# Other places for moments, factor transfers, first maximum and first turned x1 in an adaLN block's prologue

## The reference, cut to what matters

```python
mod = (silu(c) @ wmod).reshape(B, 6, 1, -1)
sa, ca, ga, sb, cb, gb = (mod[:, i] for i in range(6))
ga, gb = (2 * (g >= 0) - 1) * maximum(abs(g), 0.25)     # each gate
h = layernorm(x) * (1 + ca) + sa
q, k, v = h @ Wq.T, h @ Wk.T, h @ Wv.T                  # rank 64 shared by the heads
x = x + ga * (softmax(q @ k.T) @ v) @ Wo.T
h = layernorm(x) * (1 + cb) + sb
x = x + gb * ((h @ sum(factors)) / sqrt(8) + bias)      # 8 factors of 512 x 512
```

## Time and profile before

| | us |
|---|---|
| median of 3 runs (471.33 to 473.3) | 471.39 |
| profiled execution | 475.28 |
| its span | 473.2 |
| TensorE matmuls busy | 453.5 (96%) |
| VectorE busy | 365.2 (77%) |
| ScalarE busy | 332.1 (70%) |
| GpSimd busy | 249.9 (53%) |

### The profile page before, as it was taken

The page is one execution under the profiler, slowest core; times in us unless marked ns, Lnnn a source line. Parts: engine busy times, 40 slices in busy tenths (PEclk is TensorE's granted clock), DMA queues, the critical chain, the costliest instruction groups (busy, mean ns, idle before and its releaser), DMA issues.

```text
span 473.2 us, 7421 instructions
## 1 busy us (share of the span) xinstructions
PE 453.5 (96%) x2114; PEld 365.3 (77%) x2114; DVE 365.2 (77%) x627; ACT 332.1 (70%) x662; POOL 249.9 (53%) x317
## 2 busy tenths in 40 slices
PE   8999887989999999999999999999999999999996
PEld 3776666868888888888888888888888876777675
DVE  2896783779888778788888878888887668897665
ACT  2877735667887778687878777887877457657551
POOL 0476653535155565456464645555554466566662
PEclk9999998999999999999999999999999999999999
DMA  8968788673358646687867365777776246665612
GB/s 298 387 233 228 151 158 193 111 134 109 97 166 265 190 135 201 188 257 194 265 187 246 112 206 174 236 216 215 225 217 160 69 132 187 194 195 166 201 61 91
DMA packets 78199, 88.06 MB, mean 186 GB/s; under 512 B 4936, under 2 KB 55880, under 8 KB 78160
## 3 DMA queue, kind: packets, MB, share of 16 engines
q1 hardware_dynamic: 74208, 80.00, 54.6%
q0 software_dynamic: 3808, 7.34, 9.3%
q10 hardware_dynamic: 144, 0.26, 0.2%
HBM read 53.49 MB, written 34.10 MB: 185 GB/s over the span
## 4 chain that ended last, share of the span: by engine, by line
PE 75%; DVE 7%; issue 6%; ACT 4%; DMA 3%; POOL 3%; SPq 0%; ACTq 0%; DVEq 0%; POOLq 0%
PE ps_o L449 11%; PE ps_o L451 11%; PE ps_o L450 11%; PE ps_y L450 5%; PE ps_y L449 5%; PE ps_y L451 5%; PE ps_v L449 5%; PE ps_v L450 5%; PE ps_v L451 5%; PE ps_s L523 3%; PE ps_s L524 3%; PE ps_qk L449 2%; PE ps_t L455 2%; PE ps_qk L451 2%; PE ps_qk L450 2%
## 5 line engine op out<-in xcount | busy, mean ns | idle before, releaser
L1321 POOL TENSOR_SCALAR ve<-mv 128x1 f32<-128x1 f32 x64 | 23.4, 365 | 162.3 <-DVE mv L1077 114.3
L449 PE MATMUL ps_o<-v_lo,pt_hi 128*128 128x512 f32 x256 | 100.2, 391 | 2.4 <-DVE pt_lo L966 2.3
L450 PE MATMUL ps_o<-v_hi,pt_lo 128*128 128x512 f32 x256 | 99.7, 389 | 0.0
L451 PE MATMUL ps_o<-v_hi,pt_hi 128*128 128x512 f32 x256 | 99.6, 389 | 0.0
L966 DVE TENSOR_TENSOR h_lo<-h_f,h_hi 128x512 fp32r<-128x512 f32 (+1 forms) x67 | 51.8, 772 | 12.7 <-ACT h_hi L685 12.2
L449 PEld LDWEIGHTS ps_o<-v_lo,pt_hi 128*128 128x128 f32 x256 | 48.1, 188 | 14.7 <-issue 4.8
L451 PEld LDWEIGHTS ps_o<-v_hi,pt_hi 128*128 128x128 f32 x256 | 48.1, 188 | 10.1
L450 PEld LDWEIGHTS ps_o<-v_hi,pt_lo 128*128 128x128 f32 x256 | 48.0, 188 | 9.6
L714 ACT ACTIVATE h_f<-x1b,mod_t 128x128 f32<-128x128 f32 x120 | 53.0, 596 | 1.0 <-DVE x1b L1095 0.7
L449 PE MATMUL ps_y<-f_lo,h_hi 128*128 128x512 f32 (+1 forms) x124 | 48.5, 391 | 1.8 <-issue 1.0
L450 PE MATMUL ps_y<-f_hi,h_lo 128*128 128x512 f32 (+1 forms) x124 | 47.9, 386 | 0.0
(11 more groups left out here) (181 smaller groups left out, 1033.2 us busy)
## 6 DMA issues: line engine op xcount, KB each, us to landing
x_blocks<-xn SPq DMA_DIRECT2D x50, 256.0 KB, 2.5
p_blocks<-probs SPq DMA_DIRECT2D x24, 512.0 KB, 3.2
pb<-p_blocks SPq DMA_DIRECT2D x96, 128.0 KB, 3.2
x_ring<-in_x SPq DMA_DIRECT2D x16, 512.0 KB, 3.8
x1b<-x_blocks SPq DMA_DIRECT2D x30, 256.0 KB, 2.8
result<-x_ring SPq DMA_DIRECT2D x15, 512.0 KB, 3.0
f_sum<-in_factors POOLq DMA_DIRECT2D x14, 512.0 KB, 6.6
wmod<-in_wmod SPq DMA_DIRECT2D x12, 512.0 KB, 7.1
```

The source lines that it names most:

```text
L449: nc.tensor.matmul(acc, a_hi, b_lo, start=first, stop=False)
L450: nc.tensor.matmul(acc, a_lo, b_hi, start=False, stop=False)
L451: return nc.tensor.matmul(acc, a_hi, b_hi, start=False, stop=last)
L1321: nc.gpsimd.tensor_scalar(ve[:, one], mv[:, u, 1:2], EPS, None, ALU.add).then_inc(ve_done, 1)
```

## The change

On VectorE, `x_stats(q + 3)` goes to the head of each half of `prep_pair`, ahead of the queries' and keys' parts and of h, with a wait of its own for the normalization of tile q + 1 (whose moments had that place); in `first_scores_max`, `row_max(0)` goes ahead of `row(CB)`; in step 2, `turn_x1(0)` goes behind both `probs_rest`. On GpSimd the additions of the factors stand otherwise among of_x and the rests: among other things of_x(9) has one half of factor 4 in front of it where it had both, and the first half of factor 6 stands ahead of of_x(10). Nothing is computed otherwise.

```diff
--- before.py
+++ after.py
@@ -1109,12 +1109,14 @@
                     x1_stats(t - 1, 1 - u)
                 if u:
                     qk_rest(g + PB)
-                if t >= 2:
+                if t >= 3:
                     turn_x1(t - 2)
                 if u:
                     k_rest(g + PB)
                 probs_rest(t, 0)
                 probs_rest(t, 1)
+                if t == 2:
+                    turn_x1(0)
                 if q < T and q not in late_x_banks:
                     turn_x(q)
                 values(t + TB)
@@ -1176,6 +1178,11 @@
             def prep_pair(pair, between=None, first_scores=None, aside=None):
                 for u in range(2):
                     q = 2 * pair + u
+                    if not (u and first_scores is not None):
+                        if u:
+                            wait_alone(dve, dve_passed, x_loaded, 16 * (pair + 3))
+                        dve.wait_ge(xn_done, q + 2)
+                        x_stats(q + 3, 1 - u)
                     if u:
                         if between is not None:
                             between()
@@ -1185,10 +1192,6 @@
                     h_parts(q + 1, pair + u, 1 - u)
                     if u and first_scores is not None:
                         first_scores()
-                    else:
-                        if u:
-                            wait_alone(dve, dve_passed, x_loaded, 16 * (pair + 3))
-                        x_stats(q + 3, 1 - u)
                     values(q, prologue_v[u])
                     if aside is not None:
                         aside(q)
@@ -1249,8 +1252,8 @@
                                             ALU.add).then_inc(mod_t_done, 1)
 
             def first_scores_max():
+                row_max(0)
                 row(CB)
-                row_max(0)
                 bound_gate(GA)
 
             weight_rests(0)
@@ -1417,20 +1420,28 @@
             of_x(4, 0)
             add_factor(1)
             pool.wait_ge(mod_acc, SB + 1)
-            for k in range(1, C):
-                of_x(4 + k, k % 2)
-                wmod_rest(CB, k - 1, k)
-                add_half(2 + (k - 1) // 2, (k - 1) % 2)
+            of_x(5, 1)
+            wmod_rest(CB, 0, 1)
+            add_half(2, 0)
+            of_x(6, 0)
+            add_half(2, 1)
+            wmod_rest(CB, 1, 2)
+            of_x(7, 1)
+            add_half(3, 0)
+            wmod_rest(CB, 2, 3)
             of_x(TB, 0)
-            wmod_rest(CB, C - 1, C)
             add_half(3, 1)
-            add_factor(4)
+            wmod_rest(CB, 3, 4)
+            add_half(4, 0)
             of_x(TB + 1, 1)
+            add_half(4, 1)
             add_factor(5)
+            add_half(6, 0)
             of_x(TB + 2, 0)
-            add_factor(6)
+            add_half(6, 1)
+            add_half(7, 0)
             of_x1(0, 0)
-            add_factor(7)
+            add_half(7, 1)
             of_x(TB + 3, 1)
             of_x1(1, 1)
             pool.wait_ge(bias_loaded, 16)
```

## The result

The changed kernel is slower: 476.83 us median of 11 runs against 472.49 of 11 runs of the kernel before beside them, ratio 1.008 with a 95% interval of 1.0046 to 1.0114. The forecast was 466.2 us, in a range of 463.8 to 469.7.

What follows compares the result with a forecast made beforehand. TensorE's matmuls were taken to limit the steps, so an earlier start moves the end. Terms -0.3 - 2.0 - 1.5 - 2.0 + 0.6 = -5.2 us from 475.28, less 3.9 for the profiler, gave 466.2 (463.8 to 469.7).

Steps and rivals of the forecast that it cites:

- C: Tile 5 in the prologue: moments ahead delay h_lo, for which queries and keys wait; +0.4 us, bounds 0 and +1.0.
- D: Tile 6's h: the copy at 55.63 should run without a GpSimd rest beside it; -0.5 us, bounds 0 and -0.7.
- F: Prologue: stats(9) in front of h(7) gives back time on TensorE; +0.5 us, 0 to +1.0.
- G: Tile 9, first maximum, columns: exponentials come earlier, a 1.1 us idle time remains before tile 8's values; -2.0 us.
- H: Clock from tile 8's values to the next scores: no fall behind 1.1 us idle; -1.5 us, bounds 0 and -1.5.
- A: Pair 0, near 30 us: moments ahead push h_lo back, queries and keys wait; +1.3 us, between +0.4 and +1.7.
- B: Tile 6: moments fall where VectorE waited for k_both, removing TensorE's xn wait at 51.51; -0.7 us.
- E: Tile 8: earlier moments and GpSimd order ready nmr(8) before ScalarE asks, removing TensorE's wait at 62.14; -1.3 us.
- I: Step 2: pt_lo(2) no longer waits for the fetch, -1.6 us; the wait for xn(11) shrinks by 0.4.
- J: Step 2: ScalarE is late next, with exponentials(3) before the transposes at 111.63; +0.6 us.
- Rival 2: VectorE becomes the prologue's bound and the first wait brings a clock fall; 3.5 us less gain, 469.7 us; chance 0.12.
- Rival 3: Start comes early, but trips through memory hold the steps; part of the gain lost, about 469.5 us; chance 0.10.

Runs made afterwards that it cites:

- before again: The kernel before, unedited, executed and profiled afresh two times: 473.47 and 472.96 us.
- control without factor 7: The kernel before with both halves of factor 7 left out of the sum: 474.32 us, ratio 0.9999.
- moments-only kernel: The kernel before with only VectorE's moments of x ahead in prep_pair; GpSimd's order, first maximum and turn unchanged: 474.95 us, ratio 1.0035.
- second profile: The changed kernel, unedited, executed and profiled afresh: 478.49 us.
- rests-first kernel: The changed kernel with each of three GpSimd rests ahead of the half factor's issue instead of behind it: 476.59 us, ratio 1.0048.
- second-halves kernel: Rests-first kernel with factor 7's second half issued behind of_x(11) and moments ahead only in second halves of pairs 1 and 2: 472.51 us, ratio 0.9974.
- all-but-moments kernel: The changed kernel without its prep_pair part, so the moments keep their old place: 474.96 us, ratio 1.0021.
- GpSimd's order only: The kernel before with only the change's lines on GpSimd: 475.6 us, ratio 1.0021.

## Why the prediction was wrong

Two steps failed, of about equal size. Set against its own profile the forecast was -5.2 us and the changed kernel's profile shows +0.5 (475.75 for 475.28), 5.7 us off. Of these, 3.4 arose by the first scores (-0.3 forecast, +3.1 measured: terms C, D and F, and the clock), 0.4 by the scores of tile 1 (G and H: -3.5 forecast, -3.1 measured), 0.3 by those of tile 4 (-1.4 and -1.1), and 1.6 behind them, where nothing was forecast. The second failed step is the base: 3.9 us were taken off as the profiler's. By its own steps:

- **The base, and with it G and H.** G and H came nearly as forecast against the execution that they were read from. What failed is the 2.70 us wait and the clock of 0.66 taken as what the kernel does. The three other profiles with before's order on both engines up to there (before again twice, and the control without factor 7) have 0.85 to 1.08 us there and no fall, and reach the scores of tile 1 3.6 to 4.0 us sooner. G (-2.0) and H (-1.5) removed a stall that most executions, to judge by these and by the clocks, don't have. My rule for setting the profiled time against the median, 3.9 us "the profiler's", was the same mistake: profiled executions of before took 473.47 and 472.96 us, beside a median of 473.48 of 17 timings.
- **A.** Right in place and size: +1.3 forecast, the wait grew by 1.18 (1.89 against 0.71); the 1.6 laid out by the page of the Trainium skill was further off. Its lower bound of +0.4 does not follow from its terms: 1.0 less the 0.98 that h_lo would gain is nothing. What it lacked is the clock, which can fall behind such a wait: it did in the moments-only kernel and in the changed one's second profile (0.57 and 0.59 over 4 us, so 1.7 and 1.6 us lost).
- **C, D and F** were the mis-sized terms: +0.4 - 0.5 + 0.5. I let h be late by the length of the moments and D be a gain because the rest moved away. In the changed order three rests follow an issue, and the VectorE copies and subtractions that were caught by the pair took 1.90, 2.83 and 2.15 us. By place, C's wait was 1.83 in the first profile and 0.85 in the second; D's was 1.97 and none, where before had 0.31 and a gain was forecast; F's was none and 1.78. C's twin in pair 1, 0.83 in the second profile, was not in the sum. My bounds, 1.0 each, came from VectorE's own rows and not from GpSimd's. The h_lo of 0.69 at 50.34 that I read as alone was not alone: a rest began 0.06 us behind it, and there the rest was the one that took longer, 1.77 for 1.29 (row in the last section). The page cited at A, "SBUF — State Buffer" of the Trainium skill (section Who interferes with whom), has the rule that the shared pair is locked by one of the two engines at a time; I applied it to one stretch and not to the order of GpSimd, which the change is about. The trace agrees with it in kind: the same operations took 0.78 and 0.69 once the rests stood first. Why an issue alone holds no subtraction (0.69 at 52.08 in the rests-first kernel) and an issue with a rest behind it does, from before the rest begins, stays open.
- **B and E** were right: the waits for xn of tiles 6 and 8 are gone. They bought nothing in the changed kernel, as h_lo is late next at the same place; in the second-halves kernel, where the first wait is short again, the scores of tile 0 come 0.6 to 0.9 us before those of before again.
- **I and J.** pt_lo's wait of 1.60 is 0 to 0.69 in usual executions, so I was worth 0 to 0.7 of its 1.6. Its other 0.4, for tile 11, was not shown either way: the transfer out of x1 took 4.6 and 5.3 us in the two profiles of the changed kernel and 4.8, 5.5 and 4.9 in the three of before, so the collision was there already. In the three variants that start earlier with this order it took 5.7 to 5.8 us, and the wait grew to between 2.08 and 2.71. J was right (0.81 for 0.6).
- **The rivals.** Rival 2, VectorE as the prologue's bound with a fall of the clock, is what happened, though its D of 0 was still too good; its price was 3.5 us, on a base that lacked 3.9. Rival 1 (the clock falls again near 73 us) did not. Rival 3 was right in one point: the rests-first kernel's lead did vanish behind the prologue, in step 2, by the collision. Rival 4 did not occur; no addition was late enough to hold factor_parts in the changed kernel. Rival 5's terms add to 2.2 us, so its time is 464.0 and not 464.3.

What stays open: each profile also shows single losses of 0.4 to 1.9 us behind step 4 at places that differ from one to the next, in all kernels; their cause was not tried. Nor was it tried which of the parts of the second-halves kernel makes its 0.26%: the early maximum and the late turn were never run alone.

## What to carry to other kernels

Before forecasting the removal of a stall, ask whether it is there in most executions: one profile is one draw, and its time and granted clock beside those of the other timings hint at which kind it was. The experiments' own profiles are draws too: two of them lie 3.5 and 4.1 us above their kernel's median. When an order on GpSimd is changed, lay it against VectorE's copies and subtractions in SBUF, not only against what GpSimd waits for: an issue with a rest right behind it held them for 1.5 to 2.1 us more, a rest alone for up to 1.2. And a stage that starts earlier meets the transfers of the one before; move those too.

## What of the hardware was not expected

The same 64 x 256 copy took 0.29 us alone (changed kernel at 58.57), 0.96 beside a rest, and 2.15 beside an issue with a rest behind it; the moments' sums, with one input, took 0.66 to 0.70 in the first 125 us of every profile. An issue with nothing behind it held neither a subtraction (0.69 at 52.08 in the rests-first kernel) nor a copy (h_hi, 0.43 at 50.62 in the moments-only kernel). The rest itself is recorded with 1.71 to 1.77 us right behind an issue and 1.26 to 1.30 elsewhere, but its record then begins 0.4 us before the issue's ends, so the work need not be longer; 1.77 also stands where it began just behind the start of a subtraction on VectorE (before at 50.40):

```profile
50.40 1.77 POOL L1405 TENSOR_TENSOR w_part<-wmod,w_part 128x512 fp32r<-128x512 f32 x1
```

The clock fell behind waits of 1.50 us (GpSimd's order only, 0.88 over 56 to 60 us and 0.69 over 60 to 64) and 1.9 in some executions and stayed at 1.00 behind waits of 1.50 and 2.08 in the all-but-moments kernel: the length of the wait alone doesn't settle it.
